# A cross-attention and routed-FFN kernel: re-ordered opening, first scores and FFN weights, products with V on two row halves

## The reference, cut to what matters

```python
def xattn(hq, hkv, mask, bias, Wq, Wk, Wv, Wo):
    q, k, v = (hq @ Wq), (hkv @ Wk), (hkv @ Wv)          # 512 -> 32 heads x 128
    score = einsum('bqhd,bkhd->bhqk', q, k) / sqrt(128) + bias
    probs = softmax(where(mask, score, -inf)); probs = where(mask, probs, 0)
    return einsum('bhqk,bkhd->bqhd', probs, v).reshape(b, lq, 4096) @ Wo

def ffn(x, base_W, base_b, router_W, router_b, A, B, expert_map):
    base_out = x @ base_W.T + base_b
    p, i = top_k(softmax(x @ router_W.T + router_b), 8)   # of 15
    w = sum over k of p[k] * onehot(expert_map[i[k]], 8)
    h = einsum('btd,erd->bter', x, A)                     # 8 experts x rank 16
    return base_out + einsum('bter,eor->bto', h * w[..., None], B) * 2.0

x = x + xattn(layernorm(x), ctx, mask, bias, Wq, Wk, Wv, Wo)
x = x + ffn(layernorm(x), ...)
```

## Time and profile before

| | |
|---|---|
| median of 3 runs | 798.69 us |
| the profiled execution | 798.68 us, span 796.9 us |
| TensorE busy | 781.5 us (98%) |
| weight loads busy | 653.6 us (82%) |
| VectorE, ScalarE, GpSimd busy | 577.1, 335.2, 188.7 us |
| DMA | 118.35 MB, mean 149 GB/s |

### The profile page before, as it was taken

How to read it: one execution, slowest core, us unless ns; L and a number is a source line. 1 busy time by engine, 2 the same in 40 slices (tenths; PEclk the granted TensorE clock), 3 DMA queues, 4 the chain that set the end, 5 groups by cost and what they waited for, 6 DMA issues and landing times.

```text
span 796.9 us, 16335 instructions
## 1 busy us (share of the span) xinstructions
PE 781.5 (98%) x6366; PEld 653.6 (82%) x6366; DVE 577.1 (72%) x1047; ACT 335.2 (42%) x657; POOL 188.7 (24%) x203
## 2 busy tenths in 40 slices
PE   8899999999999999999999999999999999999998
PEld 7788888888888888778888888887888888888886
DVE  3894526247677666687987798778878888768974
ACT  4553525245555555453433244423433343314420
POOL 0052232114424434242211221222211221010200
PEclk9999999999999999999999999999999999999999
DMA  6436673234454546674563356435553555343002
GB/s 224 146 146 224 205 259 134 105 133 160 159 185 159 172 158 187 213 234 125 160 172 120 108 160 186 121 108 167 164 142 112 145 160 173 101 121 88 0 3 104
DMA packets 108074, 118.35 MB, mean 149 GB/s; under 512 B 44239, under 2 KB 77007, under 8 KB 107998
## 3 DMA queue, kind: packets, MB, share of 16 engines
q1 hardware_dynamic: 107998, 117.31, 47.0%
HBM read 81.64 MB, written 35.65 MB: 147 GB/s over the span
## 4 chain that ended last, share of the span: by engine, by line
PE 92%; DVE 4%; ACT 2%; issue 2%; DMA 1%; SPq 0%; DVEq 0%
PE pY L1378 40%; PE pP L1378 39%; PE pY L1540 4%; PE pO L1565 2%; PE pO L1378 1%; PE pT_ L1565 1%; PE pT_ L1550 1%; PE pS L1550 1%; DMA ctx<-in_ctx 1%; ACT wv_hi L646 1%; DVE y L1096 1%; DVE pr L1135 1%; PE pS L1565 1%; PE pO L1424 1%; DVE sm L1126 0%
## 5 line engine op out<-in xcount | busy, mean ns | idle before, releaser
L1096 DVE TENSOR_TENSOR y<-y,pY 128x512 f32<-128x512 f32 x124 | 84.5, 682 | 19.5 <-PE pY L1378 19.3
L1378 PE MATMUL pY<-wo_hi,oT_hi 128*128 128x512 f32 x248 | 97.2, 392 | 0.7 <-DVE y L1096 0.6
L1378 PE MATMUL pY<-wo_lo,oT_hi 128*128 128x512 f32 x248 | 96.6, 390 | 0.0
L1378 PE MATMUL pY<-wo_hi,oT_lo 128*128 128x512 f32 x248 | 96.5, 389 | 0.0
L1378 PE MATMUL pP<-xo_hi,wk_hi 128*128 128x512 f32 x210 | 83.4, 397 | 0.8 <-ACT v_s L631 0.8
L1378 PE MATMUL pP<-xo_hi,wk_lo 128*128 128x512 f32 x210 | 82.0, 390 | 0.5 <-issue 0.5
L646 ACT CAST wk_hi<-twk 128x256 fp32r<-128x256 f32 x128 | 52.1, 408 | 71.3 <-PE pP L1378 59.9
L1378 PE MATMUL pP<-xo_lo,wk_hi 128*128 128x512 f32 x210 | 81.9, 390 | 0.0
L579 POOL TENSOR_TENSOR bias<-bias,madd 128x512 f32<-128x512 f32 x32 | 43.9, 1382 | 150.3 <-DMA bias<-in_fside_Bx32xSxS 150.3
L885 DVE TENSOR_TENSOR wk_lo<-twk,wk_hi 128x256 fp32r<-128x256 f32 x128 | 58.7, 463 | 22.0 <-ACT wk_hi L646 22.0
L885 DVE TENSOR_TENSOR wk_lo<-wk_raw,wk_hi 128x256 fp32r<-128x256 f32 x96 | 45.7, 476 | 25.6 <-ACT wk_hi L646 25.4
(11 more groups left out here) (277 smaller groups left out, 1912.0 us busy)
## 6 DMA issues: line engine op xcount, KB each, us to landing
v_hbm<-stage SPq DMA_DIRECT2D x64, 256.0 KB, 2.2
k_hbm<-stage SPq DMA_DIRECT2D x64, 256.0 KB, 3.5
k<-k_hbm SPq DMA_DIRECT2D x16, 1024.0 KB, 5.4
v<-v_hbm SPq DMA_DIRECT2D x16, 1024.0 KB, 7.6
wk_raw<-in_L_xattn_Wk SPq DMA_DIRECT2D x16, 512.0 KB, 4.4
wo_raw<-in_L_xattn_Wo SPq DMA_DIRECT2D x16, 512.0 KB, 3.6
bias<-in_fside_Bx32xSxS SPq DMA_DIRECT2D x128, 64.0 KB, 3.5
wk_raw<-in_L_xattn_Wq SPq DMA_DIRECT2D x16, 512.0 KB, 4.6
```

The lines of the kernel that those rows point to most:

```text
L1096: nc.vector.tensor_tensor(y[:, t, :], y[:, t, :], src[:, :], ALU.add).then_inc(y_added, 1)
L1378: mm = nc.tensor.matmul(bank_, a, b, start=first and n == 0, stop=last and n == len(terms) - 1, skip_group_check=read_between)
```

## The change

- Opening: 14 warm-ups between the first two transposed blocks of context, none behind them (4 and 8 before). ScalarE casts `b12` and slot 5 of the first weight set ahead of the high parts of context block 4, and slots 3 and 2 one place earlier; `copy_v(1)` goes ahead of `sums_high(2)`. VectorE follows with the same order; `first_t3` and `first_t2` come ahead of slot 5 and of `sums_of_a(1)`, and in blocks of V `make_c11(n)` goes ahead of the low part of slot 0 or of slot 5 that stood before it.
- First scores: within block QA the order 6, scores, scores, 7, 5, 3, 4 becomes 6, 7, 5, scores, scores, 3, 4. On ScalarE `exp(0)` goes behind slot 4; on VectorE slots 2 and 3 come first, `make_c22` stands behind `biased(0)`, and `add_up(0)` comes after `make_c21`.
- FFN weights: `ffn_weights(4)` goes into the second half of the pair's products with Wo, `ffn_weights(6)` ahead of the last products with V; the splits follow on both engines.
- `h_and_logits` multiplies with the first 144 columns and not with all 256; the zeroes are written as before.
- `times_v` issues one matmul of 64 by 128 per row half, not two of 64 by 64.

```diff
@@ scalar, opening @@
             higher(0, 1)
+            wait_raw(act, 0, (0, 1))
+            nc.scalar.copy(b12[0][:, :, :], raw_block(0, 0, 1)).then_inc(b12_h, 1)
+            higher(0, 5)
             last_high(0)
             (a21 copy)
-            wait_raw(act, 0, (0, 1))
-            nc.scalar.copy(b12[0][:, :, :], raw_block(0, 0, 1)).then_inc(b12_h, 1)
             rows_out(1)
             last_high(1)
             piece_of_first(0, 2, pP[0], c11_made)
             copy_p1(1)
-            higher(0, 5)
+            higher(0, 3)
             sums_high(1)
             piece_of_first(2, 4, pP[1], c21_made)
-            higher(0, 3)
+            higher(0, 2)
             piece_of_first(1, 3, pP[0], c12_made)
-            higher(0, 2)
...
+            copy_v(1)
             sums_high(2)
-            copy_v(1)
@@ scalar, block QA @@
             higher(w, 2)
-            exp(0)
             higher(w, 3)
             copy_v(n)
             higher(w, 4)
+            exp(0)
             copy_c12(n)
@@ vector, opening @@
+            first_low(0)
             lower_w(0, 0)
-            first_low(0)
             first_low(1)
             lower_w(0, 1)
+            (b12 low part)
+            first_t3()
             last_low(0)
             (a21 low part)
-            (b12 low part)
+            first_t2()
+            lower_w(0, 5)
             sums_of_a(1)
-            lower_w(0, 5)
+            lower_w(0, 3)
             sums_low(1)
-            first_t3()
-            first_t2()
-            lower_w(0, 3)
             lower_w(0, 2)
@@ vector, blocks 3 to 31 @@
+                if n < NV:
+                    make_c11(n)
                 if w is not None:
                     lower_w(w, 0)
                 if late is not None:
                     lower_w(late, 5)
-                make_c11(n)
+                if n >= NV:
+                    make_c11(n)
@@ vector, block QA @@
+            lower_w(w, 2)
+            lower_w(w, 3)
             biased(0)
-            lower_w(w, 2)
+            make_c22(n)
             largest(0)
             biased(1)
             less_max(0)
             largest(1)
-            lower_w(w, 3)
             less_max(1)
-            make_c22(n)
             lower_w(w, 4)
-            add_up(0)
             lower_w(w, 5)
             make_c21(n)
+            add_up(0)
+            lower_w(w, 6)
             weights(0)
-            lower_w(w, 6)
@@ tensor @@
             turn_ctx(0, first_turn(0))
-            warm_up(4)
+            warm_up(14)
             turn_ctx(1, first_turn(1))
-            warm_up(8)
...
                 for t in range(NT):
-                    for d in range(2):
-                        for i in range(2):
-                            rows = slice(64 * i, 64 * i + 64)
-                            mm = nc.tensor.matmul(pO_of[s][i][64 * d:64 * d + 64, t * S:(t + 1) * S],
-                                                  v[rows, t, s * DH + 64 * d:s * DH + 64 * d + 64],
-                                                  pT[s][rows, t, :], start=True, stop=True)
-                            if t == NT - 1 and d == 1:
-                                mm.then_inc(o_full, 1)
+                    for i in range(2):
+                        rows = slice(64 * i, 64 * i + 64)
+                        mm = nc.tensor.matmul(pO_of[s][i][:, t * S:(t + 1) * S], v[rows, t, s * DH:(s + 1) * DH],
+                                              pT[s][rows, t, :], start=True, stop=True)
+                        if t == NT - 1:
+                            mm.then_inc(o_full, 1)
...
-            times(n, 6)
+            for p in (6, 7, 5):
+                times(n, p)
             scores(0)
             scores(1)
-            for p in (7, 5, 3, 4):
-                times(n, p)
+            times(n, 3)
+            times(n, 4)
...
             for t in range(4, NT):
                 times_wo(i, t)
+                if t == 5:
+                    ffn_weights(4)
             turn_p(h + 2)
             turn_p(h + 3)
-            ffn_weights(4)
             ffn_weights(5)
+            ffn_weights(6)
             times_v(h + 2)
             times_v(h + 3)
-            ffn_weights(6)
...
-                product(pG[t // 2][:, t % 2 * ARW:(t % 2 + 1) * ARW],
-                        [(xt, (ar[0][:, c, :], ar[1][:, c, :])) for c, xt in enumerate(xt_parts(t))]
+                product(pG[t // 2][:, t % 2 * ARW:t % 2 * ARW + GW],
+                        [(xt, (ar[0][:, c, 0:GW], ar[1][:, c, 0:GW])) for c, xt in enumerate(xt_parts(t))]
```

More of the change, by code:

```diff
@@ L25 @@
 ARW = 256
+GW = 144
 SCALE = float(DH) ** -0.5
@@ L850, in _ @@
             wo_high(NP - 1)
+            split_ffn(4)
             turned_p(h + 2)
             turned_p(h + 3)
-            split_ffn(4)
             split_ffn(5)
+            split_ffn(6)
             o_high(h + 2)
             o_high(h + 3)
-            split_ffn(6)
             for i in range(NT + 1):
@@ L1009, in first_t4 @@
                                         ).then_inc(tw_made, 1)
+            first_low(0)
             lower_w(0, 0)
-            first_low(0)
             first_low(1)
             lower_w(0, 1)
+            dve.wait_ge(b12_h, 1)
+            lower(b12[1][:, :, :], raw_block(0, 0, 1), b12[0][:, :, :], b12_l)
+            first_t3()
             dve.wait_ge(a21_h, 1)
@@ L1019, in _ @@
                   a21_l)
-            dve.wait_ge(b12_h, 1)
-            lower(b12[1][:, :, :], raw_block(0, 0, 1), b12[0][:, :, :], b12_l)
+            first_t2()
+            lower_w(0, 5)
             sums_of_a(1)
-            lower_w(0, 5)
+            lower_w(0, 3)
             sums_low(1)
-            first_t3()
-            first_t2()
-            lower_w(0, 3)
             lower_w(0, 2)
@@ L1267, in _ @@
             o_low(h + 2, 1)
-            split_ffn(4)
-            split_ffn(5)
             o_low(h + 3, 0)
             o_low(h + 3, 1)
+            split_ffn(5)
             split_ffn(6)
```

## The result

The changed kernel takes 815.47 us (median of four runs, 814.97 to 815.93) against 798.44 for the kernel before on the same chip: ratio 1.0196, interval 1.0171 to 1.0221, slower by 2%. The profiled span is 813.5, 16.6 more than before; the forecast was 816, +17.6.

What follows compares the result with a forecast made beforehand. TensorE, with 92% of the span and busy nearly everywhere, was taken as the bound; 26.1 - 3.0 - 3.2 - 0.1 - 1.6 - 0.6 = +17.6 on 798.7 gave 816 us, range 788 to 826.

Steps and rivals of the forecast that it cites:

- V, +26.1: Products with V: 16 rounds in each of 32 heads go from 0.059 to 0.110 us, adding 26.1 us.
- The estimate of 0.110 a round: V: a round of two is filled by its 128-column FP32 weight load, 0.110 us against 0.059 before.
- the bound of 0.22: V: two row halves load one after the other, 0.22 us a round, total 873; chance 0.04.
- The first rival: V: 128-column FP32 load is quick, so V adds nothing and the rest stays, total 790; chance 0.15.
- The count as the price: V: each record costs its issue, so half the records save 0.49 us a head, total 774.5; chance 0.03.
- Issue stalls, -3.0: V's bursts: of eight stops without a semaphore, 5.4 us in all, 3.0 goes; bounds 0 and -5.4.
- The opening, -3.2: Opening: earlier first product and smaller TensorE holes save 3.2 us, kept to the end; bounds +1 and -4.7.
- The wait of 0.65 for the last quarter of Wv: Opening: slot 5's cast needs that quarter, landing at 12.4; TensorE gets A21's low part at 14.95, standing 0.65.
- First scores, -0.1: Block QA: third product's 0.77 wait goes, new waits of about 0.5 and 0.2 come; bounds -0.9 and +0.7.
- FFN weights, -1.6: Last pair: TensorE's 1.68 us wait for the last transposed weight goes, saving 1.6; bounds -1.7 and 0.
- Logits, -0.6: Logits: 144 columns for 256 shorten 96 matmuls of 0.120, only the last tiles counting; saves 0.6 us.
- The rival of slow narrow products: Logits: fp32r at 144 columns runs like FP32 rows, 0.265 us each, +13.9, total 831; chance 0.06.

Runs made afterwards that it cites:

- e4: Changed kernel with each product with V moving only 32 of its 64 columns, weight loads still 128 columns: 826.64 us.
- e8: Changed kernel with V back on four 64x64 quarters, each product moving 32 of its 64 columns: 796.69 us.
- e3: Changed kernel with V as 64x64 products again, ordered so that only two quarters, one per row half, run together: 810.68 us.
- e5: Changed kernel with both V products of a round on the same row half of the array (rows 0 to 63): 942.89 us.
- e6: Changed kernel with V on four quarters and the Q block's first product moved between the two heads' products with V: 801.16 us, ratio 1.0014.
- e12: e6 with the first-scores order of the kernel before and ScalarE's first-product copy ahead of its second-head V casts: 797.22 us, ratio 0.9956.
- e2: Changed kernel with the products with V back on four quarters, all else as changed: 796.54 us, ratio 0.9963.
- e11: Kernel before with only the FFN weights moved and the logits on 144 columns: 797.98 us, ratio 0.9972.

## Why the prediction was right, step by step

- **V, +26.1.** Right in mechanism and nearly in size: 16 x 1.70 = 27.2. The estimate of 0.110 a round was read from two loads in the earlier trace rows and measured 0.111. e4 and e8 show that the moved columns don't set the round at either width, e3 that half of the loaded columns are half of the time, e5 that the row halves load side by side (the bound of 0.22 is excluded). The first rival, 790 by a quick load, fell: the transposes' load of 128 FP32 columns in the earlier trace rows is no measure for one of an ordinary FP32 matmul. The Trainium skill, "TensorE: Matmul & The Clock Gate", LDWEIGHTS (loading the stationary operand), gives columns / 1.2 ns, that is 53 and 107 ns, and the runs agree with 0.0525 and 0.111. The Trainium skill, "TensorE: Matmul & The Clock Gate", Weight-path perf modes, grants the fast load only to a type other than FP32. The FP32 load of 128 columns at 0.111 agrees with that, but no run here shows a load that gets it.
- **The count as the price** fell with e3: twice V's instructions, and 0.36 less a pair for V.
- **Issue stalls, -3.0.** Too small: 5.8 of waits went from the pair loop, over my bound of 5.4. I counted only the stops without a releaser in V; from start to start those of the loop are 3.6. With them went a stop of the same kind just behind V (0.8 with what follows, its row is below) and two waits for VectorE's additions to y, at 469.68 and 547.38 (0.6 each with what follows), since a slower V gives VectorE 1.70 more in each pair.

```profile
667.84 0.50 PE L1378 MATMUL pP<-xo_hi,wk_lo 128*128 128x512 f32 x1 [0.46 <-issue]
```

e3 and e6 show that the stops hang on how densely the instructions stand, at the same number of them. That the supply of instructions gives out was my reading, and rows that I overlooked speak for it. The profile has the loads of instructions as DMA packets of their own; the page's row (packets, MB, share) is the first below for the kernel before and the second for the changed kernel, which has 2044 instructions fewer, all of them TensorE's:

```profile
q8 instruction: 51, 0.84, 0.4%
```

```profile
q8 instruction: 43, 0.70, 0.4%
```

In the kernel before, five of the first thirteen pairs have a stop in V or just behind it. They are the five in which such a packet begins within 0.42 of V's start, before or after (at 353.41, 430.90, 508.95, 587.26 and 665.27), and TensorE goes on 2.4 to 2.7 after the packet's start (356.12, 433.49, 511.34, 589.98, 667.84). In the other eight none begins within 0.8. In e3, with V at half the density, packets begin 0.05 to 0.45 ahead of V in four pairs, and none of them stops. Its one stop (0.53, up to 353.80) has a packet 0.46 behind V's start, at 351.28. No run moved a packet, so the cause is pointed at by these rows and not shown by an experiment.
- **The opening, -3.2.** -3.58. The wait of 0.65 for the last quarter of Wv did not occur, because it landed 0.9 earlier than in the trace that I had read (e12 shows the wait where it lands late); those at 31.52 (0.77, forecast 0.65) and 33.68 (0.53, forecast 0.9) did.
- **First scores, -0.1.** The step that failed, +1.17, beyond its bound of +0.7. The two new waits were forecast at 0.5 and 0.2 and measure 0.53 and 0.47. V of the first pair also waits for its load: scores to V is 2.61 (348.43 to 351.04) where it was 2.02. I had walked the three engines and not SyncE's queue: there the bias loads that follow the first scores, now two products later in the order, start at 332.95 (333.81 before, a lead of 0.86 where TensorE had 3.58) and take 5.4, stores of K stand behind them, and the load of v, which waits 3.4 for the last of these stores to land, is issued at 345.65 and lands 5.3 later. In e2 it lands in time; the other 0.6 to 0.7 is in both. Of that 0.4 is the new waits: from start to start they cost 0.69 and 0.63, where the one that went cost 0.93. The rest isn't traced.
- **FFN weights, -1.6.** Together with the last pair's V 0.0 was forecast, -0.10 measured. e11 shows that it rests on the slower V: with quarters only 0.90 is gained, because the wait goes over to V's own result (1.12).
- **Logits, -0.6.** -0.58, by a load of 0.11 that fills the product, as with V. The rival of slow narrow products fell with the same row.

The errors of +1.0 (V in 15 pairs), -2.8 (stalls), -0.4 (opening), +1.3 (first scores) and -0.1 (last pair) largely cancel, so the margin of 1 us is in part luck: V's term is right, two of the small terms lay outside their own bounds, to opposite sides.

## What to carry to other kernels

Count weight columns, not matmuls: where FP32 products move no more columns than they load, the load fills the round, and quarters that load at the same time beat halves of twice the width. A wait that a change removes may be one of several in a row, so ask which engine behind it was nearly late as well. When an order is walked, walk the DMA queue with it.

## What the runs showed of the hardware

- Two quarters of one row half load their weights at once: four loads of 64 FP32 columns in 0.059, two in 0.0525.
- TensorE's clock fell while it was busy without a gap. With V on one row half alone (e5) the granted clock was 0.67 in the second head's stretch, behind a first head at 1.00, and records went from 0.11 to 0.21, the pace of the lower of its two levels; with 32 moved columns on both halves (e4) it held for 620 us and then was 0.81 on the mean of a stretch of V. The changed kernel, with 64 columns on both halves, keeps 1.00. Why e4 holds so long and then doesn't stays open.
- Stops without a releaser came and went with the density of instructions, up to 1.3 us each, at equal counts; in the kernel before all five of the first thirteen pairs fall where a packet of instructions begins within 0.42 of V's start.
